# A recurrent block on one core: half-size VectorE operations, silu and row statistics on ScalarE, and one operand of every odd state step on GpSimd

## Chip, cores and metric

The kernel runs on one core of one Trainium2 chip. The metric is device time in microseconds; the kernel before took 2645.11 us (median of three runs, 2644.86 to 2647.88). All data are float32.

## The reference, cut to what matters

```python
# x: (8, 2048, 512); state of 64 per batch row
xn = layernorm(x)                                   # over the 512
x_norm = layernorm(xn) * g + b
x_norm = x_norm + conv3_depthwise(x_norm) + conv_b  # over time
gate, input_gate = split(x_norm @ gate_w.T + gate_b)
Bm = (x_norm * sigmoid(input_gate)) @ B_w.T + B_b
Cm = x_norm @ C_w.T + C_b
A_bar = expm(dt_A * A)
for t in range(2048):                               # the recurrence
    s = s @ A_bar + Bm[t]
    s = layernorm64(s) * ln_st_g + ln_st_b
    y[t] = Cm[t] * s
ssm = (y @ D_w.T + D_b) * sigmoid(gate)
g = silu(xn @ W.T + b + (xn @ V_r) @ C.T)
out = x + ssm * g
```

## The kernel before, in words

Time is cut into 32 chunks of 64 steps; a chunk has 8 x 64 = 512 tokens. Everything but the recurrence is wide work on tiles of 128 partitions by 512: conv (`left_tap`, `right_tap`), the two gates, the projections B, C and D, the feed-forward part. While chunk i's 64 state steps run, the same iteration prepares chunk i+1 (its norm, conv, input gate, B and C; part "A"), makes the feed-forward and the gate of chunk i (part "F"), finishes chunk i-1 (state times C, D projection, gating, add of x; part "C") and takes statistics for a later chunk (part "S"). Four engines work, each through a queue in order, written out by hand: the tables of numbers at the top (`V_CONV`, `V_XG`, `V_G`, `PE_O`, `POOL_LN` and so on) name the step t, 0 to 63, behind which a piece of wide work stands in its engine's queue. If a piece is late, the state steps behind it in that queue are late too.

**The state step.** All of the recurrence lies in the tile `dw`, 8 partitions (the batch), one slot per step. A slot holds r (1 column, the reciprocal root of the mean square, `CR`), a constant, and three stretches of 64 columns: w (`CD:CM`, the unnormalised state), a (`CM:CM2`) and one more (`CM2:SLOT`). The normalisation is folded into r: the step's new w is r of the step before, times a stretch of the slot before, plus what stands in its own slot. Steps go in pairs:

- even step t (`even_step`): VectorE updates w (64 columns, L720) from a of the slot before; `square_sum` (L710) makes q, the sum of squares with eps; then VectorE adds r times the look-ahead product from TensorE (waiting for `p_ready`) to the other 128 columns of its slot (L724) and gives `rest_ready`.
- odd step t (`odd_step`): VectorE updates w and a in one instruction of 128 columns (L733), which waits for `r_ready` and `rest_ready`; then `square_sum`; then a transpose of w (L737), which TensorE takes for the next look-ahead: two matmuls against a precomputed power of the matrix (L973, L974).
- GpSimd in both: `step` (L347) raises q to the power -0.5 and writes r (`r_ready`). This is one instruction on 8x1. Behind it, in slots 43 to 53, stand 13 small operations on tiles of 128x4 or 128x1 for the layer norms of a later chunk (`ln_op`, L363 to L377), each of which waits for the one before.

**Wide work on VectorE** stands behind a step's last instruction and so runs while GpSimd makes the power. The conv taps, the gating products, the gated ssm, ys and the final add are each one instruction of 512 columns; silu (L672) is two of 256; the statistics (`bn_stats`, L631) are eight of 256 per chunk, with four aggregates (L643).

**ScalarE** normalises, evicts and makes sigmoids (`ffn_sigmoid` L480, `input_gate` L452, `gate_sigmoid` L485); silu is its sigmoid in `sigf` times the biased product, on VectorE.

**SP** issues loads and stores, among them the copies that bring `dtok` into `dw` (`send_d`) and w and r out of it (`send_w`).

The setup computes the matrix exponential and prepares chunk 0; then come 32 iterations with state steps and one that only finishes the last chunk.

## Time and profile before

| | us |
|---|---|
| median of three runs | 2645.11 |
| the profiled execution's own time | 2645.41 |
| its span, first to last instruction | 2643.6 |
| TensorE busy | 2503.3 (95%) |
| VectorE busy | 2155.6 (82%) |
| GpSimd busy | 1275.2 (48%) |
| ScalarE busy | 825.8 (31%) |

The time is the device's, the span goes from the first to the last instruction of the profile. Busy shares are averages. The matmuls' ends are modelled, so TensorE's share does not mean peak. Since the state steps form one chain, what counts is the spacing from one step to the next, and which engine's result arrives last in it. Times of the rows are in us from the span's start, means in ns.

### The profile page before, as it was taken

The numbers are of one execution on the slowest core, as the hardware profiler recorded it, in microseconds if no ns is written. First come the engines' busy times: TensorE is split into PE (matmuls) and PEld (weight loads), VectorE is DVE, ScalarE is ACT, GpSimd is POOL, SyncE is SP. The second block draws the span as 40 slices with busy tenths as digits, with TensorE's granted clock in tenths as the row PEclk, the third lists the DMA queues.
The fourth block names the chain that finished last, engine by engine and source line by source line (L and its number), as shares of the span: only waits on it lengthen the run. The fifth ranks groups of instructions, "written<-read, shape, count | busy, mean of one in ns | idle before, by whom it ended". The sixth has DMA issues, their size and how long they took to land.

```text
span 2643.6 us, 39815 instructions
## 1 busy us (share of the span) xinstructions
PE 2503.3 (95%) x10001; PEld 1302.1 (49%) x10001; DVE 2155.6 (82%) x9727; ACT 825.8 (31%) x1354; POOL 1275.2 (48%) x2485
## 2 busy tenths in 40 slices
PE   6899999999999999999999999999999999999986
PEld 3445554555554555544554554455545555555443
DVE  4688888888888888888888888888888888888875
ACT  3333223333223333223333233333223333223310
POOL 2355554455554455554455554455554455554442
PEclk8999999999999999999999999999999999999997
DMA  3111121122121122111122111122111122111112
GB/s 106 24 40 46 34 55 46 46 56 50 36 50 48 45 56 52 36 48 48 45 56 56 36 43 48 48 53 56 38 42 48 49 53 56 40 39 51 29 36 50
DMA packets 99778, 125.03 MB, mean 47 GB/s; under 512 B 32159, under 2 KB 48735, under 8 KB 99552
## 3 DMA queue, kind: packets, MB, share of 16 engines
q1 hardware_dynamic: 98912, 121.43, 18.6%
q8 instruction: 85, 1.39, 0.2%
q14 instruction: 141, 1.16, 0.2%
q10 hardware_dynamic: 640, 1.05, 0.2%
HBM read 71.96 MB, written 33.55 MB: 40 GB/s over the span
## 4 chain that ended last, share of the span: by engine, by line
DVE 53%; POOL 33%; issue 10%; PE 3%; DMA 0%; ACT 0%; POOLq 0%; SPq 0%; DVEq 0%
POOL dw L347 27%; DVE wq L710 14%; DVE dw L733 12%; DVE dw L720 7%; POOL ln L363 5%; DVE wT L737 4%; DVE bank L651 3%; DVE xnorm L657 3%; DVE sgT L696 3%; DVE xg L666 3%; DVE G L679 2%; DVE o L704 1%; PE bank L940 1%; DVE ys L687 1%; PE bank L880 0%
## 5 line engine op out<-in xcount | busy, mean ns | idle before, releaser
L347 POOL TENSOR_TENSOR dw<-q,minus_half 8x1 f32<-8x1 f32 x2048 | 1101.7, 538 | 1269.8 <-DVE wq L710 1255.9
L973 PEld LDWEIGHTS bank<-Mscan,wT 128*65 128x65 f32 x2046 | 217.3, 136 | 767.4 <-issue 761.3
L733 DVE SCALAR_TENSOR_TENSOR dw<-dw 8x128 f32<-8x128 f32 x1024 | 347.8, 340 | 219.7 <-POOL dw L347 203.5
L940 PE MATMUL bank<-xnorm,gateT 128*128 128x512 f32 x1024 | 506.1, 598 | 0.9 <-issue 0.9
L931 PE MATMUL bank<-xnorm,gateT 128*128 128x512 f32 x1024 | 504.6, 595 | 0.0
L973 PE MATMUL bank<-Mscan,wT 128*65 128x128 f32 x2046 | 410.3, 282 | 96.9 <-DVE wT L737 46.8
L710 DVE SCALAR_TENSOR_TENSOR wq<-dw 8x65 f32<-8x65 f32 x2048 | 443.5, 217 | 70.2
L923 PE MATMUL bank<-xnT,WT 128*128 128x512 f32 x1024 | 495.3, 594 | 0.0
L974 PE MATMUL bank<-Mscan,wT 128*65 128x128 f32 x2046 | 392.8, 274 | 0.0
L720 DVE SCALAR_TENSOR_TENSOR dw<-dw 8x64 f32<-8x64 f32 x1024 | 269.7, 263 | 130.9 <-POOL dw L347 125.6
L724 DVE SCALAR_TENSOR_TENSOR dw<-bank,dw 8x128 f32<-8x128 f32 x1024 | 342.5, 334 | 8.2 <-PE bank L974 8.0
L452 ACT ACTIVATE bank<-bank,vec 128x512 f32<-128x512 f32 x128 | 84.7, 662 | 626.1 <-PE bank L940 626.1
L974 PEld LDWEIGHTS bank<-Mscan,wT 128*65 128x65 f32 x2046 | 254.4, 139 | 0.3
L737 DVE STREAM_TRANSPOSE wT<-dw 32x64 f32<-32x64 f32 x1024 | 232.8, 227 | 0.0
L923 PEld LDWEIGHTS bank<-xnT,WT 128*128 128x128 f32 x1024 | 167.6, 191 | 95.3 <-issue 95.3
L940 PEld LDWEIGHTS bank<-xnorm,gateT 128*128 128x128 f32 x1024 | 160.8, 191 | 90.4 <-issue 89.8
L485 ACT ACTIVATE bank<-bank,vec 128x512 f32<-128x512 f32 x128 | 84.7, 662 | 385.7 <-PE bank L931 385.7
L931 PEld LDWEIGHTS bank<-xnorm,gateT 128*128 128x128 f32 x1024 | 171.1, 191 | 62.1 <-issue 62.1
L480 ACT ACTIVATE sigf<-bank,vec 128x512 f32<-128x512 f32 x128 | 87.4, 683 | 214.8 <-PE bank L923 211.0
L710 DVE DVE_READ_ACCUMULATOR wq<-dw 8x1 f32 x2048 | 145.4, 71 | 0.0
L363 POOL TENSOR_TENSOR ln<-ln,minus_half 128x1 f32<-128x1 f32 x264 | 142.2, 539 | 4.4 <-POOL ln L363 3.8
L903 PE MATMUL bank<-ident,sgT 128*128 128x128 f32 x512 | 141.2, 280 | 1.4 <-DVE sgT L696 0.8
(131 smaller groups left out, 2471.0 us busy)
## 6 DMA issues: line engine op xcount, KB each, us to landing
xc<-in_x SPq DMA_DIRECT2D x264, 128.0 KB, 2.7
out<-o SPq DMA_DIRECT2D x256, 128.0 KB, 2.3
xa<-in_x SPq DMA_DIRECT2D x248, 128.0 KB, 2.7
dw<-dtok SPq DMA_DIRECT2D x128, 96.0 KB
wtok<-dw SPq DMA_DIRECT2D x128, 33.0 KB
gateT<-in_gateT SPq DMA_DIRECT2D x1, 2048.0 KB
xa<-in_x ACTq DMA_DIRECT2D x8, 128.0 KB, 3.6
WT<-in_WT SPq DMA_DIRECT2D x1, 1024.0 KB, 6.9
```

What stands on the lines that cost most here:

```text
L347: nc.gpsimd.tensor_tensor(dw[0:B, t, CR:CR + 1], q[:], minus_half[0:B, 0:1], ALU.pow).then_inc(s["r_ready"], 1)
L363: half_power = lambda a, b, j: g.tensor_tensor(col(b, j), col(a, j), minus_half[:, j:j + 1], ALU.pow)
L710: V.scalar_tensor_tensor(out=wq[:], in0=w_eps, scalar=1.0 / S, in1=w_eps, op0=ALU.mult, op1=ALU.mult, accum_out=q[:]).then_inc(s["q_ready" ...
L720: V.scalar_tensor_tensor(out=dw[0:B, t, CD:CM], in0=dw[0:B, before, CM:CM2], scalar=r, in1=dw[0:B, t, CD:CM], op0=ALU.mult, op1=ALU.add).t ...
L724: V.scalar_tensor_tensor(out=dw[0:B, t, CM:SLOT], in0=scanP[0:B, 0:2 * S], scalar=r, in1=dw[0:B, t, CM:SLOT], op0=ALU.mult, op1=ALU.add).t ...
L733: V.scalar_tensor_tensor(out=dw[0:B, t, CD:CM2], in0=dw[0:B, before, CM:SLOT], scalar=dw[0:B, before, CR:CR + 1], in1=dw[0:B, t, CD:CM2], ...
L737: V.transpose(wT[0:32, 0:S], dw[:, t, CD:CM]).then_inc(s["wT_ready"], 1)
L923: ins = mm(mbank["ffn", m][:], WT[:, k, P * m:P * m + P], xnT[:, k, :], start=(k == 0), stop=(k == KH - 1))
L931: ins = mm(mbank["gate", m][:], gateT[:, k, P * m:P * m + P], xnorm[p][:, k, :], start=(k == 0), stop=(k == KH - 1))
L940: ins = mm(mbank["ig", m][:], gateT[:, k, H + P * m:H + P * m + P], xnorm[p][:, k, :], start=(k == 0), stop=(k == KH - 1))
L973: mm(scanP[0:WIDE, 0:2 * S], wT[:, 0:WIDE], Mscan[:, 0, :], start=True, stop=False)
L974: mm(scanP[0:WIDE, 0:2 * S], wT[:, 32:32 + WIDE], Mscan[:, 1, :], start=False, stop=True).then_inc(s["p_ready"], 1)
```

## The change

Four things are changed together. First, each 512-column operation of VectorE in the iterations becomes two of 256 columns in two slots (conv, gatings, gated ssm, add; ys in two halves by batch rows). Second, silu is made by ScalarE in one operation into G, and both sigmoids become tanh of half the argument; VectorE adds 1 while it multiplies, and the factors 0.5 are moved into B, C and the constant row of ys. Third, the row statistics of x go to ScalarE: four sums (`row_means`) and four sums of squared deviations (`row_vars`) per chunk, with accumulated outputs. Fourth, a of the odd step is made by GpSimd: `next_a` multiplies 64 columns of the slot before by r, broadcast, into a new tile `scaled`, and adds `scaled` to the 64 columns of its own slot. VectorE's odd step then updates w alone, 64 columns; the even step also waits for `a_ready`. The layer-norm operations on GpSimd stand one behind every odd step from 33 to 57, and the output transposes of TensorE two slots later.

```diff
-PE_O = range(28, 44)
+PE_O = range(30, 46)
-V_CONV = (3, 5, 7, 9, 11, 13, 17, 19)
-V_SILU = (6, 8, 12, 14, 16, 18, 20, 22)
-V_STATS = (26, 28, 30, 32, 34, 36, 38, 40)
-V_XG = (29, 33, 37, 41)
-POOL_LN = (43, 43, 43, 44, 45, 46, 47, 48, 49, 50, 51, 52, 53)
+V_CONV = (3, 4, 5, 6, 7, 8, 9, 10, 11, 12, 13, 14, 17, 18, 19, 20)
+V_XG = (29, 30, 33, 34, 37, 38, 41, 42)
+POOL_LN = range(33, 59, 2)
...
+            def next_a(i, t):
+
+                here, before = dw[0:B, t, CM:CM2], dw[0:B, t - 1, CM2:SLOT]
+                wait_for(pool, "r_ready", CT, i, t)
+                wait_for(pool, "rest_ready", PAIRS, i, t // 2 + 1)
+                nc.gpsimd.tensor_tensor(scaled[:], before, dw[0:B, t - 1, CR:CR + 1].to_broadcast([B, S]),
+                                        ALU.mult).then_inc(s["a_scaled"], 1)
+                wait_for(pool, "a_scaled", PAIRS, i, t // 2 + 1)
+                nc.gpsimd.tensor_tensor(here, scaled[:], here, ALU.add).then_inc(s["a_ready"], 1)
+
             def step(i, t):
+                if t % 2:
+                    next_a(i, t)
                 wait_for(pool, "q_ready", CT, i, t + 1)
...
+            def row_means(n):
...
+                for j in range(NJ):
+                    wait_for(act, "mean_done", NJ, n - 3, j)
+                    a_(unused[:], xa[:, j, :], ACT.Copy, scale=-1.0 / H,
+                       accum_out=sums[:, 0, j:j + 1]).then_inc(s["mean_done"], 1)
+
+            def row_vars(n):
+                for j in range(NJ):
...
+                    a_(unused[:], xa[:, j, :], ACT.Square, bias=sums[:, 0, j:j + 1],
+                       accum_out=sums[:, 1, j:j + 1]).then_inc(s["var_done"], 1)
...
-                a_(mbank["ig", m][:], mbank["ig", m][:], ACT.Sigmoid,
+                a_(mbank["ig", m][:], mbank["ig", m][:], ACT.Tanh, scale=0.5,
...
+            def ffn_silu(c, m, p):
                 wait_for(act, "ffn_mm", KH, c, m + 1)
...
+                a_(G[p][:, m, :], mbank["ffn", m][:], ACT.Silu, bias=v_("ffn_b", m)).then_inc(s["silu_done"], 1)
...
+                part = slice(TH * h, TH * (h + 1))
+                ins = V.scalar_tensor_tensor(out=xg[:, m, part], in0=mbank["ig", m][:, part], scalar=1.0,
+                                             in1=xnorm[p][:, m, part], op0=ALU.add, op1=ALU.mult)
+                if h:
+                    ins.then_inc(s["xg_done"], 1)
...
                 wait_for(dve, "r_ready", CT, i, t)
+                wait_for(dve, "a_ready", PAIRS, i, t // 2)
                 V.scalar_tensor_tensor(out=dw[0:B, t, CD:CM], in0=dw[0:B, before, CM:CM2], scalar=r,
                                        in1=dw[0:B, t, CD:CM], op0=ALU.mult, op1=ALU.add).then_inc(s["w_ready"], 1)
...
-                V.scalar_tensor_tensor(out=dw[0:B, t, CD:CM2], in0=dw[0:B, before, CM:SLOT],
-                                       scalar=dw[0:B, before, CR:CR + 1], in1=dw[0:B, t, CD:CM2],
-                                       op0=ALU.mult, op1=ALU.add).then_inc(s["w_ready"], 1)
+                r = dw[0:B, before, CR:CR + 1]
+                V.scalar_tensor_tensor(out=dw[0:B, t, CD:CM], in0=dw[0:B, before, CM:CM2], scalar=r,
+                                       in1=dw[0:B, t, CD:CM], op0=ALU.mult, op1=ALU.add).then_inc(s["w_ready"], 1)
                 square_sum(i, t)
                 V.transpose(wT[0:32, 0:S], dw[:, t, CD:CM]).then_inc(s["wT_ready"], 1)
```

How the change moves GpSimd's queue, at the first layer-norm operations inside the iterations. Before:

```order
L365 TENSOR_SCALAR ln<-mv 128x4 [waits ln_done,mv_done,xn_done]
L366 TENSOR_SCALAR ln<-mv 128x4 [waits ln_done]
L367 TENSOR_SCALAR ln<-mv 128x4 [waits ln_done]
L347 TENSOR_TENSOR dw<-q,minus_half 8x1 [waits q_ready]
L363 TENSOR_TENSOR ln<-ln,minus_half 128x1 [waits ln_done]
L347 TENSOR_TENSOR dw<-q,minus_half 8x1 [waits q_ready]
```

and with the change (L349 is the product, L352 the sum, L358 the power):

```order
L349 TENSOR_TENSOR scaled<-dw 8x64 [waits rest_ready,r_ready]
L352 TENSOR_TENSOR dw<-scaled,dw 8x64 [waits a_scaled]
L358 TENSOR_TENSOR dw<-q,minus_half 8x1 [waits q_ready]
L382 TENSOR_SCALAR ln<-sums 128x4 [waits ln_done,var_done,xn_done]
L358 TENSOR_TENSOR dw<-q,minus_half 8x1 [waits q_ready]
L349 TENSOR_TENSOR scaled<-dw 8x64 [waits rest_ready,r_ready]
L352 TENSOR_TENSOR dw<-scaled,dw 8x64 [waits a_scaled]
```

Ahead of the odd step's power now stand two operations of 8x64, one of which waits for GpSimd's own last power and the other for the first of them; a layer-norm operation stands only behind an odd step's power.

VectorE's queue in chunk 0, among state steps with wide work. Before:

```order
L733 SCALAR_TENSOR_TENSOR dw<-dw 8x128 [waits rest_ready,r_ready]
L710 SCALAR_TENSOR_TENSOR wq,q<-dw 8x65 [waits w_ready]
L737 STREAM_TRANSPOSE wT<-dw 32x64
L651 SCALAR_TENSOR_TENSOR bank<-y,vec,bank 128x512 [waits t1_done]
L720 SCALAR_TENSOR_TENSOR dw<-dw 8x64 [waits r_ready]
L710 SCALAR_TENSOR_TENSOR wq,q<-dw 8x65 [waits w_ready]
L724 SCALAR_TENSOR_TENSOR dw<-bank,dw 8x128 [waits p_ready]
L672 SCALAR_TENSOR_TENSOR G<-bank,vec,sigf 128x256 [waits sig_done]
```

and with the change:

```order
L790 SCALAR_TENSOR_TENSOR dw<-dw 8x64 [waits rest_ready,r_ready]
L765 SCALAR_TENSOR_TENSOR wq,q<-dw 8x65 [waits w_ready]
L793 STREAM_TRANSPOSE wT<-dw 32x64
L712 SCALAR_TENSOR_TENSOR xg<-bank,xnorm 128x256 [waits xnorm_done,b_mm,igs_done]
L776 SCALAR_TENSOR_TENSOR dw<-dw 8x64 [waits a_ready,r_ready]
L765 SCALAR_TENSOR_TENSOR wq,q<-dw 8x65 [waits w_ready]
L780 SCALAR_TENSOR_TENSOR dw<-bank,dw 8x128 [waits p_ready]
L712 SCALAR_TENSOR_TENSOR xg<-bank,xnorm 128x256
```

The odd step's update (L733 before, L790 now) has 64 columns in place of 128, the even step's waits for one semaphore more, and a wide operation stands as two halves behind two steps.

## Rows read from the trace of the kernel before

**Rows 1.** The page: the chain that ended last, share of the span by engine.

```profile
DVE 53%; POOL 33%; issue 10%; PE 3%; DMA 0%; ACT 0%; POOLq 0%; SPq 0%; DVEq 0%
```

**Rows 2.** One line's instructions, L347: duration ns min/median/max, first and last start.

```profile
L347 POOL TENSOR_TENSOR dw<-q,minus_half x2048: 537/538/558, 87.4 to 2621.0; 8x1 f32<-8x1 f32 x187
```

**Rows 3.** Timeline, a pair of steps: start us, us, engine, line, operation [idle before].

```profile
1343.87 0.34 DVE L724 SCALAR_TENSOR_TENSOR dw<-bank,dw 8x128 f32<-8x128 f32 x1
1344.02 0.54 POOL L347 TENSOR_TENSOR dw<-q,minus_half 8x1 f32<-8x1 f32 x1 [0.48 <-DVE wq L710]
1344.60 0.34 DVE L733 SCALAR_TENSOR_TENSOR dw<-dw 8x128 f32<-8x128 f32 x1 [0.39 <-POOL dw L347]
1344.97 0.22 DVE L710 SCALAR_TENSOR_TENSOR wq<-dw 8x65 f32<-8x65 f32 x1
...
1345.27 0.54 POOL L347 TENSOR_TENSOR dw<-q,minus_half 8x1 f32<-8x1 f32 x1 [0.71 <-DVE wq L710]
1346.45 0.54 POOL L347 TENSOR_TENSOR dw<-q,minus_half 8x1 f32<-8x1 f32 x1 [0.64 <-DVE wq L710]
```

**Rows 4.** Timeline of GpSimd and VectorE among the layer-norm operations of a middle chunk.

```profile
1330.14 0.54 POOL L347 TENSOR_TENSOR dw<-q,minus_half 8x1 f32<-8x1 f32 x1 [0.71 <-DVE wq L710]
1330.66 0.22 POOL L365 TENSOR_SCALAR ln<-mv 128x4 f32<-128x4 f32 x1
...
1331.51 0.19 POOL L367 TENSOR_SCALAR ln<-mv 128x4 f32<-128x4 f32 x1 [0.19 <-POOL ln L366]
1331.78 0.56 POOL L347 TENSOR_TENSOR dw<-q,minus_half 8x1 f32<-8x1 f32 x1
1332.32 0.54 POOL L363 TENSOR_TENSOR ln<-ln,minus_half 128x1 f32<-128x1 f32 x1
1332.38 0.34 DVE L733 SCALAR_TENSOR_TENSOR dw<-dw 8x128 f32<-8x128 f32 x1 [0.88 <-POOL dw L347]
```

**Rows 5.** Groups of VectorE's instructions by line: busy us, mean ns, idle before.

```profile
L733 DVE SCALAR_TENSOR_TENSOR dw<-dw 8x128 f32<-8x128 f32 x1024 | 347.8, 340 | 219.7 <-POOL dw L347 203.5
L720 DVE SCALAR_TENSOR_TENSOR dw<-dw 8x64 f32<-8x64 f32 x1024 | 269.7, 263 | 130.9 <-POOL dw L347 125.6 <-DMA dw<-dtok 5.3
```

**Rows 6.** Timeline of GpSimd in the setup: operations that each wait for the last.

```profile
84.89 0.20 POOL L376 TENSOR_TENSOR ln<-ln 128x4 f32<-128x4 f32 x1 [0.18 <-POOL ln L363]
85.27 0.20 POOL L377 TENSOR_TENSOR ln<-ln 128x4 f32<-128x4 f32 x1 [0.18 <-POOL ln L376]
```

**Rows 7.** Groups of GpSimd's instructions: the two memsets.

```profile
L342 POOL MEMSET dw<- 8x64 f32 x1 | 0.2, 209 | 0.0
L341 POOL MEMSET dw<- 8x1 f32 x1 | 0.1, 88 | 0.1
```

**Rows 8.** Groups of VectorE's instructions: wide work.

```profile
L672 DVE SCALAR_TENSOR_TENSOR G<-bank,vec,sigf 128x256 f32<-128x256 f32 x256 | 118.5, 463 | 0.0
L651 DVE SCALAR_TENSOR_TENSOR bank<-y,vec,bank 128x512 f32<-128x512 f32 x128 | 90.5, 707 | 0.1
```

**Rows 9.** Timeline, a 256-column operation behind an even step, and the odd update.

```profile
1309.48 0.41 DVE L631 BATCH_NORM_STATS2 stats<-xa 128x6 f32<-128x256 f32 x1
1309.93 0.34 DVE L733 SCALAR_TENSOR_TENSOR dw<-dw 8x128 f32<-8x128 f32 x1
```

**Rows 10.** ScalarE: timeline of the first input gates, and a group that reads xa.

```profile
1310.79 0.66 ACT L452 ACTIVATE bank<-bank,vec 128x512 f32<-128x512 f32 x1 [6.71 <-PE bank L940]
1315.90 0.66 ACT L452 ACTIVATE bank<-bank,vec 128x512 f32<-128x512 f32 x1 [4.45 <-PE bank L940]
...
L418 ACT ACTIVATE z<-xa,ln 128x512 f32<-128x512 f32 x128 | 96.4, 803 | 0.0
```

**Rows 11.** TensorE: timeline; the page's granted clock in 40 slices, in tenths.

```profile
1313.32 0.38 PE L973 MATMUL bank<-Mscan,wT 128*65 128x128 f32 x2
1315.70 0.41 PE L973 MATMUL bank<-Mscan,wT 128*65 128x128 f32 x2
...
PEclk8999999999999999999999999999999999999997
```

More of the change, by code:

```diff
@@ L132, in build @@
         mv = sb("mv", [P, NJ, 2])
+        sums = sb("sums", [P, 2, NJ])
+        unused = sb("unused", [P, H])
         ln = sb("ln", [P, 7, NJ])
@@ L504, in _ @@
             act.wait_ge(s["dve_cleared"], 1)
[L505 removed]
+            a_(o[0:1, 0, 0:1], ones[0:1, 0:1], ACT.Silu)
             act.wait_ge(s["consts"], 16 * 4)
@@ L570, in iteration @@
                         copy_xnT(i + 1, k)
-                    for m in range(KH):
+                    if "S" in parts:
+                        row_means(i + 3)
+                    input_gate(i + 1, 0)
+                    if "S" in parts:
+                        row_vars(i + 3)
+                    for m in range(1, KH):
                         input_gate(i + 1, m)
@@ L625, in _ @@
             dve.wait_ge(s["dve_cleared"], 1)
-            V.memset(ys[S:WIDE, :], 1.0)
+            V.memset(ys[S:WIDE, :], 0.5)
             def half_stats(n, src, j, h):
@@ L664, in gated_x @@
+            def gated_x(c, m, h, p):
+                if h == 0:
+                    wait_for(dve, "igs_done", KH, c, m + 1)
+                if m == 0 and h == 0:
                     wait_for(dve, "b_mm", 1, c, 0)
                     wait_for(dve, "xnorm_done", KH, c, KH)
-                V.tensor_tensor(xg[:, m, :], mbank["ig", m][:], xnorm[p][:, m, :],
-                                ALU.mult).then_inc(s["xg_done"], 1)
-            def silu(c, m, h, p):
-                wait_for(dve, "sig_done", KH, c, m + 1)
-                part = slice(TOK // 2 * h, TOK // 2 * (h + 1))
-                V.scalar_tensor_tensor(out=G[p][:, m, part], in0=mbank["ffn", m][:, part], scalar=v_("ffn_b", m),
-                                       in1=sigf[:, m % 2, part], op0=ALU.add, op1=ALU.mult
-                                       ).then_inc(s["silu_done"], 1)
@@ L691, in gated_ssm, with gated_silu @@
-            def gated_ssm(c, m, p):
-                wait_for(dve, "ssm_mm", KH, c, m + 1)
-                if m == 0:
+                part = slice(TH * h, TH * (h + 1))
+                ins = V.scalar_tensor_tensor(out=xg[:, m, part], in0=mbank["ig", m][:, part], scalar=1.0,
+                                             in1=xnorm[p][:, m, part], op0=ALU.add, op1=ALU.mult)
+                if h:
+                    ins.then_inc(s["xg_done"], 1)
+            def gated_silu(c, m, h, p):
+                if h == 0:
+                    wait_for(dve, "gates_done", KH, c, m + 1)
+                    wait_for(dve, "silu_done", KH, c, m + 1)
+                part = slice(TH * h, TH * (h + 1))
+                ins = V.scalar_tensor_tensor(out=G[p][:, m, part], in0=mbank["gate", m][:, part], scalar=1.0,
+                                             in1=G[p][:, m, part], op0=ALU.add, op1=ALU.mult)
+                if h:
+                    ins.then_inc(s["g_done"], 1)
@@ L694, in gated_ssm @@
+            def gated_ssm(c, m, h, p):
+                if h == 0:
+                    wait_for(dve, "ssm_mm", KH, c, m + 1)
+                if m == 0 and h == 0:
                     wait_for(dve, "g_done", KH, c, KH)
                     wait_for(dve, "ofill", NJ, c, 0)
-                V.tensor_tensor(sgT[:, m, :], mbank["ssm", m][:], G[p][:, m, :],
-                                ALU.mult).then_inc(s["sg_done"], 1)
-            def add_x(c, j):
-                wait_for(dve, "ofill", NJ, c, j + 1)
-                wait_for(dve, OUT[j], 16 * BJ, c, 0)
-                if j == 0:
+                part = slice(TH * h, TH * (h + 1))
+                ins = V.tensor_tensor(sgT[:, m, part], mbank["ssm", m][:, part], G[p][:, m, part], ALU.mult)
+                if h:
+                    ins.then_inc(s["sg_done"], 1)
@@ L703, in add_x @@
+            def add_x(c, j, h):
+                if h == 0:
+                    wait_for(dve, "ofill", NJ, c, j + 1)
+                    wait_for(dve, OUT[j], 16 * BJ, c, 0)
+                if j == 0 and h == 0:
                     wait_for(dve, "xc_in", 16 * B, c, 16 * B)
-                V.tensor_tensor(o[:, j, :], tbank["o", j][:], xc[:, j, :],
-                                ALU.add).then_inc(s["o_done"], 1)
+                part = slice(HH * h, HH * (h + 1))
+                ins = V.tensor_tensor(o[:, j, part], tbank["o", j][:, part], xc[:, j, part], ALU.add)
+                if h:
+                    ins.then_inc(s["o_done"], 1)
@@ L744, in _ @@
             link(V.tensor_scalar(vec[:, vcol["conv_w1"], :], vec[:, vcol["conv_w1"], :], 1.0, None, ALU.add))
+            gates = slice(vcol["gate_b"], vcol["in_gate_b"] + 1)
+            link(V.tensor_scalar(vec[:, gates, :], vec[:, gates, :], 0.5, None, ALU.mult))
+            link(V.tensor_scalar(sm("C_b"), sm("C_b"), 0.5, None, ALU.mult))
             assert done[0] == SETUP_VEC
@@ L805, in _ @@
                 if n in DVE_XG0:
-                    gated_x(0, DVE_XG0.index(n), 0)
+                    for h in range(2):
+                        gated_x(0, DVE_XG0.index(n), h, 0)
             link(V.tensor_reduce(absrow[:, 5:6], XX[:, 0, :], AX_X, ALU.add))
@@ L815, in _ @@
             for m in range(len(DVE_XG0), KH):
-                gated_x(0, m, 0)
+                for h in range(2):
+                    gated_x(0, m, h, 0)
             dve.wait_ge(s["pe_setup"], SQ_END + 1)
```

168 lines of the change are left out of this document (86 added, 82 removed).

## The prediction, made before the changed kernel ran

> **What bounds the kernel now.** I read the page first, for which engine the chain that ended last runs through. VectorE holds 53% of it and GpSimd 33%, TensorE, the busiest engine, 3% [rows 1]. The chain is the recurrence: 2048 state steps, each of which needs the one before. Then the line of the step's power on GpSimd: its first start is at 87.4 us and its last at 2621.0 us, so the 2047 intervals take 2533.6 of the 2643.6 us and average 1.238 us, with 87.4 us of setup ahead and 22.6 us of drain behind [rows 2]. The median of the runs is 2645.11 us, the profiled execution's own time 2645.41, its span 2643.6; my sum is made for that execution, so 1.8 us are added to a span, and the median lies 0.3 us lower.
>
> Third, the timeline of one pair of steps where nothing is in the way [rows 3]. The power of an even step starts at 1344.02 and takes 0.54; VectorE starts the odd step's update of 128 columns at 1344.60 (0.34), the sum of squares at 1344.97 (0.22, and 0.07 for reading it out), and the next power starts at 1345.27: 1.25 us from power to power. From odd to even the update has 64 columns and the interval is 1346.45 - 1345.27 = 1.18. A pair's floor is 2.43 us. The difference to 2 x 1.238 is 0.046 us per pair, 47 us in all; it comes from places like the three layer-norm operations in one slot, which stretch an interval of odd to even to 1331.78 - 1330.14 = 1.64 us instead of 1.18 [rows 4], and from 512-column operations of up to 0.71 us [rows 8] that end just after the power does.
>
> **The change, part by part.** (a) *The odd step's update on VectorE* halves, from a row of 340 ns to one of 263 ns [rows 5]. Alone this is worth 0.077 x 1024 = 79 us: the odd power could start 1.25 - 0.08 = 1.17 us after the even one.
>
> (b) *What GpSimd now does ahead of the odd power.* Its queue is in order, so the power of the odd step stands behind a broadcast product and a sum, each 8x64. The product waits for the power of the step before (its own result) and for `rest_ready`, which is not late: the update that gives it ends at 1343.87 + 0.34 = 1344.21, and the power ends at 1344.56 [rows 3]. No row has such a product, so I build the path from spacings of starts:
> - power to an operation that waits for it: 0.54 + 0.18 = 0.72 us, the power and the idle time until GpSimd goes on after a wait for a power of its own [rows 3, 6].
> - product to the sum that waits for it: 85.27 - 84.89 = 0.38 between two operations of 128x4 [rows 6], that is 0.20 and 0.18.
> - sum to a power that doesn't wait for it: 0.27, from the last small operation at 1331.51 to the power at 1331.78 [rows 4].
> - the 60 further elements of each. GpSimd's memset of 8x64 took 209 ns and that of 8x1 88 [rows 7]: 121 ns for 63 elements, 0.115 us for 60.
>
> The sum is 0.72 + 0.38 + 0.27 + 2 x 0.115 = 1.60. The third term may be too dear, since behind a longer operation the next starts 0.02 us before its recorded end (1330.14 + 0.54 against 1330.66 [rows 4]); then it is 0.19 + 0.115 - 0.02 = 0.285 and not 0.385. I take the middle, **1.55 us** from even to odd. VectorE would have its q ready at 1.17, so the gain of 79 us in (a) is lost: the release that comes last for the odd power is no longer q, but GpSimd's own queue.
>
> The bounds of this interval: with elements that cost nothing, and the lower third term, 0.72 + 0.38 + 0.17 = 1.27; with each element three times the memset's (two inputs and an output, each at 121 ns), 0.72 + 0.38 + 0.27 + 2 x 0.346 = 2.06. I stay with one memset's price since it is the row of the very shape; 1.55 lies nearer the low end. The Trainium skill ("GPSIMD Engine Reference", section "Performance versus the Vector engine") gives about 2.6 cycles per element at 1.2 GHz for a two-input operation; an estimate from that page is 0.13 us for 60 elements, and my interval would be 1.58, some 30 us more in all. The same page's warning against elementwise work on GpSimd speaks against the change.
>
> (c) *Odd to even* keeps 1.18: power, update of 64, sum of squares are the same. The further wait for `a_ready` is met before the power's own, since GpSimd's queue gives them in that order.
>
> (d) *Halves on VectorE.* Conv, gating, gated ssm, o and ys stand as 800 more instructions. A half STT took 463 ns, a whole 707 [rows 8], so a split costs 2 x 0.463 - 0.707 = 0.22 us of VectorE, some 175 us busy in all, against 118.5 for silu and 256 statistics at 0.41, 105 us, taken off. None of it is on the path: before, such a statistic began at 1309.48, ended at 1309.89, and the next update followed at 1309.93 [rows 9]; a half of 0.46 there would end at 1309.94. What covers the halves is the power (0.54) and, in odd slots, 0.38 us more that VectorE now waits. So the 47 us of late intervals mostly go (each term above uses the clean intervals); I keep 5.3 us for waits for DMA landings [rows 5].
>
> (e) *Layer-norm operations on GpSimd* now stand behind odd powers only, one per slot, ahead of an even power. A layer-norm power of 0.54 [rows 4] there fits, since from an odd power's end to the next start GpSimd has 1.18 - 0.54 = 0.64 [rows 3]. Nothing is added, and the triple slot goes.
>
> (f) *ScalarE* gets four row sums and four sums of squares per chunk at about 0.80 us (a row of that shape from `xa`, 803 ns [rows 10]): 6.4 us. It idled 6.71 us ahead of the first input gate and 4.45 ahead of the second [rows 10], and the means stand in the first gap (3.2), the squares in the second (3.2). Silu costs it what its sigmoid did. Cost nothing; without that cover VectorE would wait at slot 29 for the gate.
>
> (g) *TensorE*: the same matmuls. Its fullest pairs take 1315.70 - 1313.32 = 2.38 us [rows 11], below 2.73. The granted clock is at the upper level (2.4 GHz) in all slices but the first and the last, where the kernel starts and drains [rows 11]. TensorE will be busy up to 87% of a pair, and its gaps are under 0.4 us each, so I take no fall of it.
>
> (h) Ends: setup and drain have some ten more splits in line, 3 us.
>
> **Sum**: 1024 x 1.55 + 1023 x 1.18 = 2794.3; + 87.4 + 22.6 + 3 + 5.3 = 2912.6 of span; + 1.8 = 2914.4. Forecast **2915 us**, 10% slower than before.
>
> **Rivals.**
> 1. *GpSimd and VectorE get in each other's way.* In odd steps the update (0.26) and the sum of squares (0.22) would run while the product and the sum do. If one waits for the end of the other: the product starts behind the update, 0.30 after the power instead of 0.18, ends at 0.61; the sum of squares takes till 0.83, the sum of a till 1.14; interval 1.70, total 2915 + 0.15 x 1024 = **3070 us**. Against: at 1332.38 an update of 8x128 started 0.06 after a layer-norm power on GpSimd and took its usual 0.34 [rows 4, 5]. The Trainium skill ("SBUF — State Buffer", section "Who interferes with whom") says a VectorE instruction with two SBUF inputs and a GpSimd one that reads SBUF fully block each other; this trace's row does not show it. 0.12.
> 2. *Elements are dear on GpSimd*: a broadcast operand or the third stream costs more than a memset's. From 1.76 us an interval on, up to 2.06: **3130 to 3440 us**. For it: pow of one element takes 0.54, so the software is slow; against: an operation of 128x4 takes 0.20 [rows 6]. 0.08.
> 3. *GpSimd keeps up* (the other side). If the product does not pay the 0.18 behind its own power, and elements cost nearly nothing, product and sum take 0.19 + 0.18 + 0.19 = 0.56, less than the 0.63 that VectorE needs; the bound goes back to VectorE and the pair falls to 2.35. TensorE then ends last at 2.38: 1024 x 2.38 + 87.4 + 22.6 + 3 + 5.3 + 1.8 = **2557 us**. It decides where the two operations with their waits take under 0.63. Every wait of GpSimd for itself in the trace shows the 0.18 [rows 6]. 0.08. Between this and my forecast lie the values near the low bound (1.27 gives 2628 us, 1.29 the time of before): 0.02 that it ends within 0.2% of before.
> 4. The rest, 0.70, is my forecast with its own terms.
>
> **Numbers.** The forecast's own spread: an element at half the memset's price and the low third term, 1.55 - 0.115 - 0.05 = 1.385, gives 2746; 60% above it and the high term, 1.74, gives 3110. Range 2750 to 3120, which takes in rival 1. Left out: rival 3 and most of rival 2. Within 0.2% (5 us, about what measurement can tell) 0.02, faster 0.08, slower 0.90.
>
> **What would show it.** In the profile after: the power's line from about 89 to 2890 us; GpSimd rows of 8x64 near 0.31 us, the sum starting 0.49 after the product, and the odd power ending its wait on GpSimd's own queue, with no idle ahead of it; VectorE waiting about 0.9 us for the power ahead of even updates where no half stands there; the chain going through GpSimd for far more than 33%. If product and sum last 0.19, or if the product starts right behind the power, (b) is wrong. If VectorE's small updates are longer than 263 ns in odd steps, rival 1 holds. If VectorE waits for ScalarE at the gates, (f) is wrong.

## The result and the profile after

The changed kernel takes 2828.99 us, median of four runs (2827.4 to 2835.08), against 2644.99 before: a ratio of 1.069, interval 1.068 to 1.071. It is 184 us slower, 7%. The forecast was 2915 us with a range of 2750 to 3120. The profiled execution took 2835.08 us itself, with a span of 2833.3.

The page's busy time, chain and clock, and then the line of the power (duration ns min/median/max, first and last start), which answer to [rows 1, 2, 11]:

```profile
PE 2570.9 (91%) x10001; PEld 1284.1 (45%) x10001; DVE 2304.2 (81%) x9913; ACT 1007.5 (36%) x1834; POOL 1882.0 (66%) x4533
POOL 47%; DVE 35%; issue 13%; PE 3%; POOLq 0%; DMA 0%; SPq 0%; ACT 0%; DVEq 0%
...
PEclk9999999999999999999999999999999999999997
```

```profile
L358 POOL TENSOR_TENSOR dw<-q,minus_half x2048: 537/538/552, 90.8 to 2810.6; 8x1 f32<-8x1 f32 x187
```

The 2047 intervals now take 2810.6 - 90.8 = 2719.8 us, 186 more than the 2533.6 of before. The span grew by 190; the other 3.4 us lie ahead of the first power, which starts at 90.8 instead of 87.4. That place moves without the change: in the kernels below it lies between 86.6 and 90.3 us, also among those with the same setup. So the loss is in the intervals, and the clock of TensorE has no part in it.

A pair of steps in the timeline, to be laid beside [rows 3]; L349 is GpSimd's product, L352 its sum, L790 and L776 VectorE's updates of the odd and the even step, L765 the sum of squares:

```profile
1362.97 0.54 POOL L358 TENSOR_TENSOR dw<-q,minus_half 8x1 f32<-8x1 f32 x1 [0.65 <-DVE wq L765]
1363.55 0.41 DVE L790 SCALAR_TENSOR_TENSOR dw<-dw 8x64 f32<-8x64 f32 x1 [0.39 <-POOL dw L358]
1363.59 0.28 POOL L349 TENSOR_TENSOR scaled<-dw 8x64 f32<-8x64 f32 x1
1363.95 0.31 POOL L352 TENSOR_TENSOR dw<-scaled,dw 8x64 f32<-8x64 f32 x1
1363.98 0.35 DVE L765 SCALAR_TENSOR_TENSOR wq<-dw 8x65 f32<-8x65 f32 x1
...
1364.43 0.54 POOL L358 TENSOR_TENSOR dw<-q,minus_half 8x1 f32<-8x1 f32 x1 [0.17 <-DVE wq L765]
...
1365.00 0.28 DVE L776 SCALAR_TENSOR_TENSOR dw<-dw 8x64 f32<-8x64 f32 x1 [0.19 <-POOL dw L358]
1365.31 0.22 DVE L765 SCALAR_TENSOR_TENSOR wq<-dw 8x65 f32<-8x65 f32 x1
...
1365.61 0.54 POOL L358 TENSOR_TENSOR dw<-q,minus_half 8x1 f32<-8x1 f32 x1 [0.65 <-DVE wq L765]
```

From even to odd power it is 1364.43 - 1362.97 = 1.46 us instead of 1.25, from odd to even 1.18 as before. 0.21 x 1024 = 215 us; the late intervals from odd to even of before, now mostly shorter, give 27 back. The reader is to see two things. The odd power waits 0.17 us and is released by VectorE's q, so GpSimd's own queue, which has ended its sum at 1364.26, is not last. And q is late because two VectorE instructions are long: the odd update takes 0.41 us where the even one of the same shape takes 0.28, and the odd sum of squares 0.35 where the even one takes 0.22. Each of them runs beside one of GpSimd's two new operations. The groups say the same for the whole run (busy us, mean ns, idle before):

```profile
L790 DVE SCALAR_TENSOR_TENSOR dw<-dw 8x64 f32<-8x64 f32 x1024 | 414.6, 405 | 125.2 <-POOL dw L358 92.0
L776 DVE SCALAR_TENSOR_TENSOR dw<-dw 8x64 f32<-8x64 f32 x1024 | 282.2, 276 | 264.0 <-POOL dw L358 212.2 <-issue 15.1 <-DMA dw<-dtok 5.3
L712 DVE SCALAR_TENSOR_TENSOR xg<-bank,xnorm 128x256 f32<-128x256 f32 x256 | 99.1, 388 | 0.0
...
L352 POOL TENSOR_TENSOR dw<-scaled,dw 8x64 f32<-8x64 f32 x1024 | 316.6, 309 | 80.3
L349 POOL TENSOR_TENSOR scaled<-dw 8x64 f32<-8x64 f32 x1024 | 290.2, 283 | 86.4 <-DVE dw L780 6.0
```

The idle time ahead of GpSimd's product is 86.4 us for 1024 of them, 0.084 each; the layer-norm operations, which also wait for GpSimd's own last result, have 0.18 [rows 6].

**Theories.** A: GpSimd's reading of SBUF holds up VectorE instructions beside it, and that makes the interval. B: the interval is GpSimd's queue, as I forecast, and VectorE's long records are a side effect. C: the halves and ScalarE's new work have a part in the loss.

### The profile page after: what moved, and what is told of

It is laid out like the page before. It is cut to its first block, busy times and chain, and to the rows that moved or that the text cites. A ratio compares the mean times of both kernels' runs of the same rounds, so it can differ in the third digit from the quotient of the medians.

```text
span 2833.3 us, 44471 instructions
## 1 busy us (share of the span) xinstructions
PE 2570.9 (91%) x10001; PEld 1284.1 (45%) x10001; DVE 2304.2 (81%) x9913; ACT 1007.5 (36%) x1834; POOL 1882.0 (66%) x4533
## 3 DMA queue, kind: packets, MB, share of 16 engines
q14 instruction: 177, 1.45, 0.2%
## 4 chain that ended last, share of the span: by engine, by line
POOL 47%; DVE 35%; issue 13%; PE 3%; POOLq 0%; DMA 0%; SPq 0%; ACT 0%; DVEq 0%
POOL dw L358 39%; DVE wq L765 15%; DVE dw L776 10%; DVE dw L790 9%; POOL dw L352 4%; POOL scaled L349 4%; PE bank L997 1%; PE bank L937 0%; POOLq L217 0%; PE bank L1030 0%; PE bank L1023 0%; PE bank L1062 0%; PE bank L1049 0%; PE bank L1031 0%; DMA xc<-in_x 0%
## 5 line engine op out<-in xcount | busy, mean ns | idle before, releaser
L358 POOL TENSOR_TENSOR dw<-q,minus_half 8x1 f32<-8x1 f32 x2048 | 1103.2, 539 | 688.7 <-DVE wq L765 661.8
L765 DVE SCALAR_TENSOR_TENSOR wq<-dw 8x65 f32<-8x65 f32 x2048 | 587.3, 287 | 70.7
L1030 PEld LDWEIGHTS bank<-Mscan,wT 128*65 128x65 f32 x2046 | 199.3, 136 | 960.6 <-issue 960.4
L790 DVE SCALAR_TENSOR_TENSOR dw<-dw 8x64 f32<-8x64 f32 x1024 | 414.6, 405 | 125.2 <-POOL dw L358 92.0
L776 DVE SCALAR_TENSOR_TENSOR dw<-dw 8x64 f32<-8x64 f32 x1024 | 282.2, 276 | 264.0 <-POOL dw L358 212.2
L352 POOL TENSOR_TENSOR dw<-scaled,dw 8x64 f32<-8x64 f32 x1024 | 316.6, 309 | 80.3
L349 POOL TENSOR_TENSOR scaled<-dw 8x64 f32<-8x64 f32 x1024 | 290.2, 283 | 86.4 <-DVE dw L780 6.0
L1031 PEld LDWEIGHTS bank<-Mscan,wT 128*65 128x65 f32 x2046 | 254.5, 139 | 0.1
L513 ACT ACTIVATE G<-bank,vec 128x512 f32<-128x512 f32 x128 | 87.5, 684 | 231.2 <-PE bank L980 227.4
```

Of the source, the lines that this page charges most:

```text
L349: nc.gpsimd.tensor_tensor(scaled[:], before, dw[0:B, t - 1, CR:CR + 1].to_broadcast([B, S]), ALU.mult).then_inc(s["a_scaled"], 1)
L352: nc.gpsimd.tensor_tensor(here, scaled[:], here, ALU.add).then_inc(s["a_ready"], 1)
L358: nc.gpsimd.tensor_tensor(dw[0:B, t, CR:CR + 1], q[:], minus_half[0:B, 0:1], ALU.pow).then_inc(s["r_ready"], 1)
L765: V.scalar_tensor_tensor(out=wq[:], in0=w_eps, scalar=1.0 / S, in1=w_eps, op0=ALU.mult, op1=ALU.mult, accum_out=q[:]).then_inc(s["q_ready" ...
L776: V.scalar_tensor_tensor(out=dw[0:B, t, CD:CM], in0=dw[0:B, before, CM:CM2], scalar=r, in1=dw[0:B, t, CD:CM], op0=ALU.mult, op1=ALU.add).t ...
L790: V.scalar_tensor_tensor(out=dw[0:B, t, CD:CM], in0=dw[0:B, before, CM:CM2], scalar=r, in1=dw[0:B, t, CD:CM], op0=ALU.mult, op1=ALU.add).t ...
```

## Experiments

The kernel before took 2642.85 to 2647.56 us (medians) beside these. Line numbers differ a little from kernel to kernel.

### The parts alone

The change without GpSimd's part:

```diff
             def step(i, t):
-                if t % 2:
-                    next_a(i, t)
...
-                V.scalar_tensor_tensor(out=dw[0:B, t, CD:CM], in0=dw[0:B, before, CM:CM2], scalar=r,
-                                       in1=dw[0:B, t, CD:CM], op0=ALU.mult, op1=ALU.add).then_inc(s["w_ready"], 1)
+                V.scalar_tensor_tensor(out=dw[0:B, t, CD:CM2], in0=dw[0:B, before, CM:SLOT],
+                                       scalar=dw[0:B, before, CR:CR + 1], in1=dw[0:B, t, CD:CM2],
+                                       op0=ALU.mult, op1=ALU.add).then_inc(s["w_ready"], 1)
```

> The change without its part on GpSimd: a of the odd step is again made by VectorE in its update of 128 columns; halves, silu and statistics on ScalarE stay. Theory A (GpSimd's product and sum stretch VectorE's two small operations of the odd step from 0.26 and 0.22 to 0.41 and 0.36 us, and so move q from 1.17 to 1.46 us behind the even power): without them the interval from even to odd power is 1.25 us again, odd to even 1.18, 2.43 a pair, about 90.8 + 2047 intervals of 1.215 + 24 = 2602 us plus few us of slot effects, 2600 to 2615 us, faster than before. Theory B (the halves or ScalarE's new work are part of the loss, by late wide work): the intervals stay above 1.25 and the time is at or above the 2645 of before.

It took 2620.94 us, ratio 0.990 (0.989 to 0.992): faster than before by 26 us (1%), 6 us above the range that I gave. So the halves and ScalarE's new work gain a little and lose nothing: theory C falls. Even to odd is 1.25 again; per chunk it takes 78.2 us, before 79.1 (spacing of the powers 64 steps apart). The triple layer-norm slot and the late 512-column operations are gone; what is left over 32 x 2.43 = 77.8 is 0.06 at each of the four steps that wait for a copy into `dw` and 0.04 at two layer-norm slots.

The kernel before with GpSimd's part alone:

```diff
             def step(i, t):
+                if t % 2:
+                    next_a(i, t)
...
                 wait_for(dve, "r_ready", CT, i, t)
+                wait_for(dve, "a_ready", PAIRS, i, t // 2)
...
-                V.scalar_tensor_tensor(out=dw[0:B, t, CD:CM2], in0=dw[0:B, before, CM:SLOT],
...
+                V.scalar_tensor_tensor(out=dw[0:B, t, CD:CM], in0=dw[0:B, before, CM:CM2], scalar=r,
```

> The kernel before with only a of the odd step moved to GpSimd; wide work, silu and statistics as before. Theory A: even to odd 1.46 us instead of 1.25, so 2645 + 0.21 x 1024 = 2860 us, and the loss is the GpSimd part's alone. Theory B (the halves are needed or harmful for it): if the halves cause part of the 1.46, the interval here is shorter and the time lies near 2750 us.

2876.22 us, ratio 1.087 (1.085 to 1.088), 16 us more than I expected, and 1.46 us again from even to odd, so the interval owes nothing to the halves. The excess is in the slots of the layer norm: some 120 intervals from even to odd take 1.67 to 1.69. Timeline of GpSimd there (L360 is the power, L376 a layer-norm power, L351 and L354 product and sum):

```profile
1360.47 0.56 POOL L360 TENSOR_TENSOR dw<-q,minus_half 8x1 f32<-8x1 f32 x1
1361.01 0.54 POOL L376 TENSOR_TENSOR ln<-ln,minus_half 128x1 f32<-128x1 f32 x1
1361.06 0.27 DVE L748 SCALAR_TENSOR_TENSOR dw<-dw 8x64 f32<-8x64 f32 x1 [0.87 <-POOL dw L360]
1361.52 0.28 POOL L351 TENSOR_TENSOR scaled<-dw 8x64 f32<-8x64 f32 x1
1361.88 0.31 POOL L354 TENSOR_TENSOR dw<-scaled,dw 8x64 f32<-8x64 f32 x1
1362.16 0.54 POOL L360 TENSOR_TENSOR dw<-q,minus_half 8x1 f32<-8x1 f32 x1
```

A layer-norm power behind an even power pushes product, sum and the odd power: 1362.16 - 1360.47 = 1.69 us. Here the queue is last, and VectorE's update (L748), with the product far away, takes 0.27. The change's table of slots, behind odd powers only, avoids that.

### What in GpSimd's two operations does it

Two memsets in their places, same waits:

```diff
-                nc.gpsimd.tensor_tensor(scaled[:], before, dw[0:B, t - 1, CR:CR + 1].to_broadcast([B, S]),
-                                        ALU.mult).then_inc(s["a_scaled"], 1)
+                nc.gpsimd.memset(scaled[:], 0.0).then_inc(s["a_scaled"], 1)
                 wait_for(pool, "a_scaled", PAIRS, i, t // 2 + 1)
-                nc.gpsimd.tensor_tensor(here, scaled[:], here, ALU.add).then_inc(s["a_ready"], 1)
+                nc.gpsimd.memset(scaled[:], 0.0).then_inc(s["a_ready"], 1)
```

> The change with GpSimd's product and sum replaced by two memsets of 8x64 into the scratch tile, with the same waits and in the same places in the queue. Left out: a of the odd step is not updated with r times the slot before. Theory A, in the form that it is GpSimd's reading of SBUF that holds up VectorE's instructions with two SBUF inputs: VectorE's odd update is 0.26 us and its sum of squares 0.22, the interval 1.17, the pair 2.35 or TensorE's 2.38, 2545 to 2575 us. Theory C (any GpSimd instruction at that time, or its semaphores, stretches VectorE's): the odd update stays near 0.40 and the time near 2800. Theory D (GpSimd's queue alone set the 1.46): as A in time, but VectorE's durations in the change would then have been no part of it.

2560.02 us, ratio 0.967 (0.965 to 0.969), as theory A had it. Timeline:

```profile
1360.96 0.28 DVE L789 SCALAR_TENSOR_TENSOR dw<-dw 8x64 f32<-8x64 f32 x1
...
1360.98 0.14 POOL L349 MEMSET scaled<- 8x64 f32 x1
1361.18 0.14 POOL L351 MEMSET scaled<- 8x64 f32 x1
1361.27 0.22 DVE L764 SCALAR_TENSOR_TENSOR wq<-dw 8x65 f32<-8x65 f32 x1
```

The first memset starts where the product started, the update takes 0.28 and the interval is 1.18 to 1.19. So the waits and semaphores of the new part stretch nothing. That the memsets spare VectorE because they only write is not shown: they are also short. In the kernels below a held instruction ends 0.07 to 0.09 us behind GpSimd's; held like that by a memset that ends at 1361.12, the update would be through at 1361.20, ahead of its own end at 1361.24, and the sum of squares (1361.40 against 1361.49) likewise. Nor does this run tell theory A from B, since the memsets shorten GpSimd's queue as well.

The product alone:

```diff
-                                        ALU.mult).then_inc(s["a_scaled"], 1)
-                wait_for(pool, "a_scaled", PAIRS, i, t // 2 + 1)
-                nc.gpsimd.tensor_tensor(here, scaled[:], here, ALU.add).then_inc(s["a_ready"], 1)
+                                        ALU.mult).then_inc(s["a_ready"], 1)
```

> The change without GpSimd's sum; the product alone stands ahead of the odd power. Left out: a of the odd step does not get the product. Theory A, each GpSimd operation stretching the VectorE instruction that it runs beside: the odd update stays at 0.41, the sum of squares falls back to 0.22, the interval to 1.32 and the time to 2829 - 0.14 x 1024 = 2685 us. If the stretch were one thing for both, it stays at 2829 or falls to 2560.

2685.99 us, where theory A had 2685, with an interval of 1.32; both lines' instructions (duration ns min/median/max):

```profile
L788 DVE SCALAR_TENSOR_TENSOR dw<-dw x1024: 262/406/411, 89.8 to 2664.1; 8x64 f32<-8x64 f32 x171
L763 DVE SCALAR_TENSOR_TENSOR wq<-dw x2048: 215/216/220, 88.9 to 2664.6; 8x65 f32<-8x65 f32 x187
```

The update is stretched as before, no sum of squares is. Each GpSimd operation costs time in the one VectorE instruction beside it: the product 0.13 us of interval (1.32 against 1.19 with memsets), the sum 0.14 (1.46 against 1.32).

Product and sum on one column, then two copies of 8x64:

```diff
-                nc.gpsimd.tensor_tensor(scaled[:], before, dw[0:B, t - 1, CR:CR + 1].to_broadcast([B, S]),
+                nc.gpsimd.tensor_tensor(scaled[:, 0:1], before[:, 0:1], dw[0:B, t - 1, CR:CR + 1],
                                         ALU.mult).then_inc(s["a_scaled"], 1)
...
-                nc.gpsimd.tensor_tensor(here, scaled[:], here, ALU.add).then_inc(s["a_ready"], 1)
+                nc.gpsimd.tensor_tensor(here[:, 0:1], scaled[:, 0:1], here[:, 0:1], ALU.add).then_inc(s["a_ready"], 1)
```

> The change with product and sum on one column instead of 64, same waits and places. Left out: 63 of 64 columns of a. If what holds VectorE up lasts as long as GpSimd's reading and no longer, one element stretches nothing: update 0.27, sum of squares 0.22, interval about 1.18, 2560 us. If it lasts as long as the GpSimd instruction (about 0.19 with one element), VectorE's instructions are stretched by a part of it and the time lies at 2600 to 2700.

```diff
-                nc.gpsimd.tensor_tensor(scaled[:], before, dw[0:B, t - 1, CR:CR + 1].to_broadcast([B, S]),
-                                        ALU.mult).then_inc(s["a_scaled"], 1)
+                nc.gpsimd.tensor_copy(scaled[:], before).then_inc(s["a_scaled"], 1)
                 wait_for(pool, "a_scaled", PAIRS, i, t // 2 + 1)
-                nc.gpsimd.tensor_tensor(here, scaled[:], here, ALU.add).then_inc(s["a_ready"], 1)
+                nc.gpsimd.tensor_copy(scaled[:], here).then_inc(s["a_ready"], 1)
```

> The change with product and sum replaced by two GpSimd copies of 8x64 from the same places into the scratch tile: one input each instead of two. Left out: a of the odd step is not updated. If any reading of SBUF by GpSimd holds VectorE up, the stretch is there while a copy reads, with a shorter duration: update 0.27 to 0.40, time between 2560 and 2829, about 2650. If only GpSimd instructions with two inputs do it, it is gone: 2560.

They took 2586.12 and 2653.64 us, intervals of 1.22 and 1.28. Timeline of the first, then of the second:

```profile
1360.85 0.30 DVE L790 SCALAR_TENSOR_TENSOR dw<-dw 8x64 f32<-8x64 f32 x1
1360.89 0.18 POOL L349 TENSOR_TENSOR scaled<-dw 8x1 f32<-8x1 f32 x1
```

```profile
1363.05 0.33 DVE L789 SCALAR_TENSOR_TENSOR dw<-dw 8x64 f32<-8x64 f32 x1 [0.39 <-POOL dw L357]
1363.08 0.23 POOL L349 COPY scaled<-dw 8x64 f32<-8x64 f32 x1
1363.36 0.23 POOL L351 COPY scaled<-dw 8x64 f32<-8x64 f32 x1
1363.41 0.26 DVE L764 SCALAR_TENSOR_TENSOR wq<-dw 8x65 f32<-8x65 f32 x1
```

A GpSimd operation with one input is enough to hold VectorE up, for less time. In all three kernels the update ends 0.07 to 0.09 us behind the end of the GpSimd operation beside it: 1363.96 against 1363.87 in the change, 1361.15 against 1361.07 with one column, 1363.38 against 1363.31 with the copy. So the stretch goes with GpSimd's duration. My alternatives for one column, nothing or 2600 us and more, were both off: the operation is shorter (0.18) than most of the update, so 0.02 to 0.03 us is all that is left of the effect.

VectorE's odd update with its first input in PSUM:

```diff
-                V.scalar_tensor_tensor(out=dw[0:B, t, CD:CM], in0=dw[0:B, before, CM:CM2], scalar=r,
-                                       in1=dw[0:B, t, CD:CM], op0=ALU.mult, op1=ALU.add).then_inc(s["w_ready"], 1)
+                V.scalar_tensor_tensor(out=dw[0:B, t, CD:CM], in0=scanP[0:B, 0:S], scalar=r,
+                                       in1=dw[0:B, t, CD:CM], op0=ALU.max, op1=ALU.min).then_inc(s["w_ready"], 1)
```

> The change with VectorE's odd update reading its first input from PSUM instead of SBUF (and max and min for product and sum), so that it has one SBUF input; GpSimd's product and sum stay as they are. Left out: w of the odd step is not the reference's. If only VectorE instructions with two SBUF inputs are held up, the update takes 0.28 to 0.32 us instead of 0.41 although the product runs beside it, the sum of squares then reads between the product and the sum or beside the sum, and the interval is between GpSimd's own path, 0.54 + 0.08 + 0.28 + 0.08 + 0.31 - 0.04 = 1.25 us, and 1.46: 2614 to 2829 us, nearer the low end. If inputs play no part, the update stays at 0.41 and the time at 2829.

2624.94 us, near the low end of the 2614 to 2829 that I gave. GpSimd's operations are those of the change, in the same places:

```profile
1362.63 0.54 POOL L358 TENSOR_TENSOR dw<-q,minus_half 8x1 f32<-8x1 f32 x1 [0.65 <-DVE wq L765]
...
1363.20 0.27 DVE L790 SCALAR_TENSOR_TENSOR dw<-bank,dw 8x64 f32<-8x64 f32 x1
1363.24 0.28 POOL L349 TENSOR_TENSOR scaled<-dw 8x64 f32<-8x64 f32 x1
1363.51 0.22 DVE L765 SCALAR_TENSOR_TENSOR wq<-dw 8x65 f32<-8x65 f32 x1
1363.60 0.31 POOL L352 TENSOR_TENSOR dw<-scaled,dw 8x64 f32<-8x64 f32 x1
...
1363.88 0.54 POOL L358 TENSOR_TENSOR dw<-q,minus_half 8x1 f32<-8x1 f32 x1
```

With one SBUF input the update takes 0.27 beside a product of 0.28. It still writes to SBUF, so it is its second SBUF input, and not its output, that makes it wait in the change. The sum of squares, still with two, starts 0.09 us ahead of GpSimd's sum, between the two operations, and keeps its 0.22. Now no idle time stands ahead of the power: this is GpSimd's queue as the bound, and its path is 1.25 us, not the 1.55 of my sum. That settles theory B: in the change the queue alone would have allowed 1.25, and q comes at 1.46. It also shows that the move could gain nothing even if nothing were held up: 2624.94 us here, 2620.94 with the halves alone.

This is what the Trainium skill says ("SBUF — State Buffer", section "Who interferes with whom"): a VectorE instruction with two SBUF inputs contends with a GpSimd one that reads SBUF, and not with one that only writes; one with at most one SBUF input, outside VectorE's two-port modes, does not contend. By that rule, the traces agree on VectorE's side: 0.41 us with two SBUF inputs, 0.27 with one. On GpSimd's side product, sum and copy all read and all write, and the memsets are too short, so that it is the reading rests on the skill. The same section says that issue order decides who blocks. In the records of the traces that order is not to be seen: the update's starts 0.04 us ahead of the product's, and the update is the one that took longer. Nor is a GpSimd instruction always in the way until its end: the layer-norm power of 0.54 us left the update beside it at its usual length [rows 4], and the one of the second experiment does the same. Those powers started 0.05 to 0.06 us ahead of the update, which alone does not explain it, since GpSimd's sum also starts 0.03 ahead of the sum of squares that it holds up.

### Why GpSimd's own path was shorter than I took it

The layer-norm operations have one more instruction, `hold`, a semaphore increment between wait and work. The change with it:

```diff
+                hold(pool)
                 nc.gpsimd.tensor_tensor(scaled[:], before, dw[0:B, t - 1, CR:CR + 1].to_broadcast([B, S]),
...
+                hold(pool)
                 nc.gpsimd.tensor_tensor(here, scaled[:], here, ALU.add).then_inc(s["a_ready"], 1)
```

> The change with one more instruction on GpSimd, a semaphore increment, between the wait and the operation, ahead of the product and ahead of the sum, as the layer-norm operations have it. It tests why the gap behind a wait of GpSimd for itself is 0.08 us in the changed kernel and was 0.18 in the layer-norm rows. If the increment is the difference, the gaps become 0.18, the product starts 0.72 us after the even power, the sum ends at about 1.49 and the odd power starts at 1.49 to 1.57: 2829 + 0.03 to 0.11 x 1024 = 2860 to 2940 us, with GpSimd's queue last and no wait for q. If the difference has another cause, the gaps stay at 0.08 and the time at 2829.

2856.53 us, with an interval of 1.48 (I had 2860 to 2940 and 1.49 to 1.57, just missed). Timeline:

```profile
1361.98 0.54 POOL L360 TENSOR_TENSOR dw<-q,minus_half 8x1 f32<-8x1 f32 x1
...
1362.56 0.27 DVE L792 SCALAR_TENSOR_TENSOR dw<-dw 8x64 f32<-8x64 f32 x1
1362.73 0.28 POOL L350 TENSOR_TENSOR scaled<-dw 8x64 f32<-8x64 f32 x1 [0.20 <-POOL dw L360]
1362.86 0.23 DVE L767 SCALAR_TENSOR_TENSOR wq<-dw 8x65 f32<-8x65 f32 x1
...
1363.19 0.31 POOL L354 TENSOR_TENSOR dw<-scaled,dw 8x64 f32<-8x64 f32 x1 [0.18 <-POOL scaled L350]
...
1363.46 0.54 POOL L360 TENSOR_TENSOR dw<-q,minus_half 8x1 f32<-8x1 f32 x1
```

The gaps are 0.20 and 0.18 instead of 0.08, so `hold` costs 0.12 and 0.10 us. The product now starts 0.17 us behind the update, and VectorE's instructions are back at 0.27 and 0.23. Almost the same interval as in the change comes from the other bound: here the queue is last, there q was.

### A version that keeps the gain

The short update is worth having only if a costs nothing elsewhere. VectorE can make it itself behind the transpose, where the power covers it; the rest of the change stays:

```diff
             def step(i, t):
-                if t % 2:
-                    next_a(i, t)
...
                 square_sum(i, t)
                 V.transpose(wT[0:32, 0:S], dw[:, t, CD:CM]).then_inc(s["wT_ready"], 1)
+                V.scalar_tensor_tensor(out=dw[0:B, t, CM:CM2], in0=dw[0:B, before, CM2:SLOT], scalar=r,
+                                       in1=dw[0:B, t, CM:CM2], op0=ALU.mult, op1=ALU.add).then_inc(s["a_ready"], 1)
```

> The change with a of the odd step made by VectorE, but as an instruction of its own of 64 columns behind the sum of squares and the transpose, where the power covers it; GpSimd makes the power alone. All of the reference is computed. Theory A says that the gain of the shorter odd update (0.08 us a pair) is there once nothing of GpSimd's contends: interval 1.17 to 1.19, pair 2.35 to 2.38, as in the write-only run: 2560 us, 2550 to 2575, 3% faster than before. Rival: the third piece behind an odd step (0.26) makes the half behind it late in the 24 of 32 pairs that have one; the half would end 0.02 to 0.08 us behind the power, and the time lies at 2580 to 2610.

2559.08 us, ratio 0.968 (0.966 to 0.969): 3.2% faster than before, and faster than the change without GpSimd's part. Timeline:

```profile
1361.61 0.55 POOL L356 TENSOR_TENSOR dw<-q,minus_half 8x1 f32<-8x1 f32 x1 [0.41 <-DVE wq L763]
...
1362.65 0.23 DVE L791 STREAM_TRANSPOSE wT<-dw 32x64 f32<-32x64 f32 x1
1362.80 0.54 POOL L356 TENSOR_TENSOR dw<-q,minus_half 8x1 f32<-8x1 f32 x1 [0.64 <-DVE wq L763]
1362.81 0.24 DVE L792 SCALAR_TENSOR_TENSOR dw<-dw 8x64 f32<-8x64 f32 x1
1362.98 0.40 DVE L710 SCALAR_TENSOR_TENSOR xg<-bank,xnorm 128x256 f32<-128x256 f32 x1
...
1363.38 0.31 DVE L774 SCALAR_TENSOR_TENSOR dw<-dw 8x64 f32<-8x64 f32 x1
1363.42 0.19 POOL L382 TENSOR_SCALAR ln<-sums 128x4 f32<-128x4 f32 x1
```

a (L792) starts with the power and the half behind it ends at 1363.38, just as the next update begins. Even to odd is 1.18 to 1.19, a pair 2.37. The last two rows show the same contention in small, as it stands in the change and in the halves alone too: two layer-norm operations of a chunk start 0.04 to 0.05 us behind an even update, and that update takes 0.31 instead of 0.27.

The same split in the kernel before, with its 512-column operations:

```diff
-                V.scalar_tensor_tensor(out=dw[0:B, t, CD:CM2], in0=dw[0:B, before, CM:SLOT],
-                                       scalar=dw[0:B, before, CR:CR + 1], in1=dw[0:B, t, CD:CM2],
+                V.scalar_tensor_tensor(out=dw[0:B, t, CD:CM], in0=dw[0:B, before, CM:CM2], scalar=r,
+                                       in1=dw[0:B, t, CD:CM],
...
                 V.transpose(wT[0:32, 0:S], dw[:, t, CD:CM]).then_inc(s["wT_ready"], 1)
+                V.scalar_tensor_tensor(out=dw[0:B, t, CM:CM2], in0=dw[0:B, before, CM2:SLOT], scalar=r,
+                                       in1=dw[0:B, t, CM:CM2], op0=ALU.mult, op1=ALU.add).then_inc(s["a_ready"], 1)
```

> The kernel before with only the odd update split on VectorE: w in 64 columns, then sum of squares, transpose, and a in 64 columns; wide work in 512 columns, silu and statistics as before. All of the reference is computed. It tells what the split needs from the halves. Theory A: the interval from even to odd falls to 1.18 (80 us less in all), but behind odd steps the 512-column operation now starts 0.16 later and ends 0.2 us behind the power: 24 intervals from odd to even of a chunk grow from 1.18 or 1.24 to about 1.40, 24 x 0.2 x 32 = 150 us more: 2700 to 2720 us. If the split alone is the gain and the halves play no part: 2565 us.

2723.12 us, ratio 1.028 (1.027 to 1.030), a little above the 2700 to 2720 of theory A:

```profile
1362.57 0.54 POOL L347 TENSOR_TENSOR dw<-q,minus_half 8x1 f32<-8x1 f32 x1 [0.65 <-DVE wq L710]
1362.58 0.24 DVE L739 SCALAR_TENSOR_TENSOR dw<-dw 8x64 f32<-8x64 f32 x1
1362.75 0.67 DVE L666 TENSOR_TENSOR xg<-bank,xnorm 128x512 f32<-128x512 f32 x1
1363.35 0.27 DVE L721 SCALAR_TENSOR_TENSOR dw<-dw 8x64 f32<-8x64 f32 x1
```

The whole operation ends at 1363.42 where the power ended at 1363.11, and the interval is 1.38 instead of 1.18 (1.45 behind a conv tap). So the split needs the rest of the change: the split alone costs 76 us, the rest alone gains 26, together they gain 84. That it is the halves that it needs is read from this timeline; no run has the split and the halves without ScalarE's new work.

## Why the prediction was right, and where it was not

- **Sign and size** were right: slower, 2829 in 2750 to 3120, by 184 us where I forecast 270. The mechanism was not, so the size is right by luck, as (b) and rival 1 show.
- **(a), the short update**, 79 us if nothing takes it back: right. The run with memsets and the split on VectorE both have an interval of 1.18 to 1.19 where I had 1.17.
- **(b), the release that comes last.** Wrong. I let GpSimd's queue be last, at 1.55 us. Three terms were off. The gap behind a wait of GpSimd for itself is 0.08 us and not 0.18, since the rows that I took it from had a semaphore increment in the gap; that is 0.20 for two. The sum to the power is 0.28 from start to start although the sum takes 0.31, and I had taken 0.335. Only the price of the elements was right: 0.283 and 0.309 for product and sum, where I had 0.305. The path is 0.616 + 0.360 + 0.277 = 1.25 (medians), which the run with the PSUM input shows as the bound. The memset row came out as a good stand-in for elements, in part by luck: it writes one column of each of 64 slots and took 0.21, while the contiguous memset of 8x64 in the third experiment took 0.14. The setup row was a bad stand-in for the gap.
- **Rival 1, contention**, to which I gave 0.12, is what happened, with another victim. I had the product wait for the update, an interval of 1.70 and 3070 us; the update waited for the product, and the sum of squares for the sum, 0.13 and 0.14 us. My row against it [rows 4] was a layer-norm power on one column; it leaves VectorE alone where a product does not, and so was no test. I named the Trainium skill's rule and then set too little by it. That 1.46 lies near 1.55 is two errors that cancel: the path too long by 0.30, the contention left out.
- **(c)** right, 1.18. **(d)** right that the halves cost nothing, shown by the run without GpSimd's part; of the 47 us of late intervals 27 went, where I had nearly all go. **(e)** right, and the second experiment shows what the old slots would have cost, 1.69 us an interval. **(f)** right: the statistics cost ScalarE more than I took, 0.82 to 0.91 us with 0.19 for reading the sum out, but VectorE waits for no gate (idle 0.0 ahead of L712). **(g)** right. **(h)** can't be told: the 3 us are within what the first power moves by among kernels with the same setup, 86.6 to 90.8.
- **The signs that I gave**: durations near 0.31 came true, and so did the chain through GpSimd, 47% instead of 33%, though it told nothing of what bounds the interval. The sum 0.49 us behind the product (0.36) and no idle time ahead of the odd power (0.17, released by q) did not come, and these two were the ones that told the mechanism. The sign that I had set for rival 1, small updates longer than 263 ns in odd steps, came: 405 ns.
